# Attention output products of six units, each as three products of rounded operands

## The reference

```
xn  = layernorm(layernorm(x)) * g1 + b1
q   = xn @ Wq                          # 16 heads x 64
k,v = split(xn @ Wkv)                  # one head of 64 each
attn = softmax(q k^T / 8)              # per head, 512 x 512
out  = concat_heads(attn @ v)          # 512 x 1024
x = x + layernorm(out @ Wo) * g2 + b2  # Wo: 1024 x 128
x = x + moe(layernorm(x))              # top 2 of 8 experts, F = 512
```

## Time and profile before

| | us |
|---|---|
| median of 3 executions | 604.21 (603.86 to 606.01) |
| profiled execution | 605.66 |
| span of its trace | 603.7 |

### The profile page before, as it was taken

One profiled execution on the slowest core, in us unless ns is written; L12 is line 12 of the kernel. 1 busy time (PEld: TensorE's weight loads), 2 busy tenths in 40 slices (PEclk: granted clock), 3 DMA queues, 4 the chain that ended last, 5 costly groups with the idle time before them and its releaser, 6 DMA issues. The chain is left out here.

```text
span 603.7 us, 8807 instructions
## 1 busy us (share of the span) xinstructions
PE 571.4 (95%) x2543; PEld 326.3 (54%) x2543; DVE 399.3 (66%) x875; ACT 297.8 (49%) x559; POOL 393.8 (65%) x329
## 2 busy tenths in 40 slices
PE   8799999999999999998999999899998898899992
PEld 6464455444545554444545545444443577788882
DVE  4878656657756869774567777876485458444463
ACT  3235655545636564463556445355635564355541
POOL 6448776667758866798598568949745944345332
PEclk9889999999999999998999999999998999999997
DMA  5111012010201200062000000000004410231042
GB/s 167 71 72 71 2 71 75 0 73 1 75 1 72 74 2 1 7 233 81 1 3 2 1 1 25 16 2 3 11 0 119 119 31 23 58 91 47 19 141 89
DMA packets 27805, 29.46 MB, mean 49 GB/s; under 512 B 7763, under 2 KB 19285, under 8 KB 27760
## 3 DMA queue, kind: packets, MB, share of 16 engines
q1 hardware_dynamic: 25056, 24.27, 12.5%
q0 software_dynamic: 2272, 4.24, 2.1%
q10 hardware_dynamic: 432, 0.39, 0.2%
HBM read 13.50 MB, written 15.32 MB: 48 GB/s over the span
## 5 line engine op out<-in xcount | busy, mean ns | idle before, releaser
L1203 ACT ACTIVATE prob<-s_ps 128x512 f32<-128x512 f32 x256 | 150.8, 599 | 183.3 <-PE s_ps L1300 180.9
L1123 DVE TENSOR_REDUCE less_max<-max_ps 128x1 fp32r<-128x512 f32 x256 | 174.0, 689 | 81.0 <-PE max_ps L1278 78.6
L1049 POOL TENSOR_TENSOR fold<-prob 128x1024 f32<-128x1024 f32 x63 | 149.6, 2375 | 88.7 <-ACT prob L1203 88.0
L1314 PE MATMUL pv_ps<-prob,v 128*64 128x512 f32 x512 | 138.5, 621 | 0.0
L1298 PE MATMUL s_ps<-q_hl,khh 128*128 128x512 f32 x256 | 117.9, 460 | 0.7 <-ACT prob L1203 0.7
L1278 PE MATMUL max_ps<-khh,q_hl 128*128 128x512 f32 x256 | 103.0, 408 | 5.4 <-DVE less_max L1123 4.8
L1300 PE MATMUL s_ps<-q_hm,kly 65*128 65x512 f32 x256 | 101.9, 398 | 0.0
L1298 PEld LDWEIGHTS s_ps<-q_hl,khh 128*128 128x128 f32 x256 | 48.6, 190 | 85.8 <-ACT prob L1203 67.1
L1055 POOL TENSOR_TENSOR psums<-fold 128x512 f32<-128x512 f32 x63 | 80.8, 1282 | 4.9
L1278 PEld LDWEIGHTS max_ps<-khh,q_hl 128*128 128x128 f32 x256 | 49.1, 192 | 23.4 <-DVE less_max L1123 11.1
L1300 PEld LDWEIGHTS s_ps<-q_hm,kly 65*128 65x128 f32 x256 | 48.8, 191 | 9.2 <-issue 3.3
(11 more groups left out here) (252 smaller groups left out, 772.0 us busy)
## 6 DMA issues: line engine op xcount, KB each, us to landing
sorted_rows<-raw_w SPq DMA_DIRECT2D x36, 260.0 KB, 2.6
raw_w<-in_gate_upT SPq DMA_DIRECT2D x8, 512.0 KB, 8.5
wd<-in_downT SPq DMA_DIRECT2D x8, 256.0 KB, 4.1
raw_w<-parts SPq DMA_DIRECT2D x6, 256.0 KB, 3.4
psums<-sorted_rows SPq DMA_DIRECT2D x22, 65.0 KB, 1.9
...
```

The lines of the kernel that those rows point to most:

```text
L1049: nc.gpsimd.tensor_tensor(fold[:, :, :], prob[:, head % 4, 0:2, :], prob[:, head % 4, 2:4, :], ALU.add).then_inc(prob_folded, 1)
L1123: nc.vector.tensor_reduce(less_max[:, group % 2, col:col + 1], max_ps[:, k % 2, :], AX_X, ALU.max, negate=True).then_inc(max_done, 1)
L1203: nc.scalar.activation(prob[:, head % 4, jt, :], s_ps[:, k % 2, :], ACT.Exp, scale=SCALE).then_inc(exp_done, 1)
L1314: last = nc.tensor.matmul(pv_ps[DH * hd:DH * hd + DH, :], v[:, b % 2, jt, :], prob[:, head % 4, jt, :], start=(jt == 0), stop=(jt == JT - 1))
```

## The change

For units 0 to 5 (24 of the 32 pairs) the OUT product is taken as three products of rounded operands (float32r), as Q is. Wo is split once into a high and a low part (`woh`, `wol`) by GpSimd, one of 8 pieces after each of the heads 2 to 9. In NORM, VectorE multiplies twice, first into `hl[:, 0]` (rounded, the high part) and then into `ao` (float32). A new step LOW on GpSimd subtracts the first from the second into `hl[:, 1]`. `ao` is free again when LOW has read it, so VectorE's NORM of pair k now waits for LOW of pair k-2. `hl` has three slots. NORM moves to slots 14, 16, 19, 21; LOW stands at 18, 18, 22, 22; OUT at 21, 23, 25, 27. Unit 6's NORM and OUT move to the same slots and keep the one float32 product; the last unit is as before. The new tiles lie over the place of the last four experts' `gate_up` weights, so these four are loaded after unit 5's last OUT.

```
-NORM_AT = (14, 17, 19, 22)
-OUT_LAG = 5
+NORM_AT = (14, 16, 19, 21)
+LOW_AT = (18, 18, 22, 22)
+OUT_AT = (21, 23, 25, 27)
+HL_SLOTS = 3
+FIRST_WEIGHTS = 4
+SPLIT_UNITS = 6
...
                 if k >= 2:
-                    dve.wait_ge(out_mm, k - 1)
+                    if k - 2 < SPLIT_UNITS * UP:
+                        dve.wait_ge(al_ready, k - 1)
+                    else:
+                        dve.wait_ge(out_mm, k - 1)
+                if u < SPLIT_UNITS:
+                    if k >= HL_SLOTS:
+                        dve.wait_ge(out_mm, k - HL_SLOTS + 1)
+                    nc.vector.tensor_tensor(hl[:, 0, k % HL_SLOTS, :], sum_ps[:, :], raw[:, k % RAW_SLOTS, :],
+                                            ALU.mult).then_inc(ah_ready, 1)
                 nc.vector.tensor_tensor(ao[:, k % 2, :], sum_ps[:, :], raw[:, k % RAW_SLOTS, :],
                                         ALU.mult).then_inc(ao_ready, 1)
...
+                slot = k % HL_SLOTS
+                if u >= SPLIT_UNITS:
+                    pe.wait_ge(ao_ready, k + 1)
+                    nc.tensor.matmul(y_ps[:, :], wof[:, c, :], ao[:, k % 2, :], start=c == 0,
+                                     stop=c == PAIRS - 1).then_inc(out_mm, 1)
+                else:
+                    pe.wait_ge(wo_split, min(k, PAIRS - 1) + 1)
+                    pe.wait_ge(ah_ready, k + 1)
+                    nc.tensor.matmul(y_ps[:, :], woh[:, c, :], hl[:, 0, slot, :], start=c == 0, stop=False)
+                    nc.tensor.matmul(y_ps[:, :], wol[:, c, :], hl[:, 0, slot, :], start=False, stop=False)
+                    pe.wait_ge(al_ready, k + 1)
+                    nc.tensor.matmul(y_ps[:, :], woh[:, c, :], hl[:, 1, slot, :], start=False,
+                                     stop=c == PAIRS - 1).then_inc(out_mm, 1)
...
-                        for e in range(E):
+                        for e in range(FIRST_WEIGHTS):
                             load_gate_up(sp, e)
+                    if (kind, u, a) == ("OUT", SPLIT_UNITS - 1, UP - 1):
+                        sp.wait_ge(out_mm, SPLIT_UNITS * UP)
+                        for e in range(FIRST_WEIGHTS, E):
+                            load_gate_up(sp, e)
...
+                        if 2 <= head < 2 + PAIRS:
+                            if head == 2:
+                                pool.wait_ge(wo_in, 16)
+                            part = head - 2
+                            link_pool(pool, nc.gpsimd.tensor_scalar(woh[:, part, :], wof[:, part, :], 1.0, 1.0, ALU.mult,
+                                                                    ALU.mult))
+                            nc.gpsimd.tensor_tensor(wol[:, part, :], wof[:, part, :], woh[:, part, :].bitcast(F32),
+                                                    ALU.subtract).then_inc(wo_split, 1)
+                    if kind == "LOW":
+                        k = u * UP + a
+                        slot = k % HL_SLOTS
+                        if k >= HL_SLOTS:
+                            pool.wait_ge(out_mm, k - HL_SLOTS + 1)
+                        pool.wait_ge(ao_ready, k + 1)
+                        pool.wait_ge(ah_ready, k + 1)
+                        nc.gpsimd.tensor_tensor(hl[:, 1, slot, :], ao[:, k % 2, :], hl[:, 0, slot, :].bitcast(F32),
+                                                ALU.subtract).then_inc(al_ready, 1)
```

26 lines of the change are left out of this document (16 added, 10 removed).

## The result

The changed kernel takes 612.81 us (median of 6, 610.76 to 613.96) against 603.84 (median of 6, 602.38 to 606.01) for the kernel before on the same chip: ratio 1.0136, 95% interval 1.0117 to 1.0155, so slower. By the two profiled executions it is 612.48 against 605.66, by their spans 610.7 against 603.7. The forecast, 607.9, had the side and not the size, and the time lies above its range (up to 611.5).

The account below looks back on a forecast made before the run. TensorE was taken to bound the kernel, working 372.1 of 378.0 us. Terms -3.4 (20 OUTs), +0.8 (unit 2), +3.0 (unit 4) and +3.3 (unit 6) gave +3.7: 607.9 us against the median 604.21, 8-in-10 range 600.3 to 611.5.

Parts of the forecast that it names:

- TensorE's gain: Three rounded products take 0.70 us where the float32 product takes 0.87, so each of 24 OUTs gains 0.17, 4.1 in all.
- the new places change nothing in this: Moving the OUTs to new slots, all behind PV, leaves TensorE's gain of 0.17 us an OUT as it is.
- the term of -3.4: The gain of the 20 OUTs outside the two stopped stretches, 0.17 us each, 3.4 us saved.
- no cost where VectorE doesn't wait: VectorE's 24 added products of 0.69 us, 16.6 in all, are hidden by its idle time: 113 of 378 us.
- Unit 2: XL up to 0.9 us later delays LOW; VectorE done at 166.8, TensorE needs it at 166.1: +0.8 us, bounds 0 and 1.6.
- Unit 4: First LOW behind XL and SEND stops OUT 1 and NORM 4, half clock one stretch later: slot 24 at 284.6, +3.0 us.
- Unit 6: First LOW behind a late SEND stops OUT 1 and NORM 4, then LIST0 stops MAX 23: slot 24 at 393.3, +3.3 us.
- The third, 2.3 for LIST0: In unit 6 LIST0 meets GpSimd's fold, pushed later by LOW, and TensorE stands 2.3 us before MAX 23.
- I take 0: A fall of the clock in unit 6 would cost about 1.6 us, bounds 0 and 3.2; it was counted as 0.
- Unit 7: No cost was counted for the moved NORM and OUT of unit 6's pairs, which run here: 0 us.
- Rival C: Larger stops: clock fall in unit 6 (+1.6), VectorE's two-input steps held up more by GpSimd (+2): 611.5 us, chance 0.10.
- Rivals A and B: A: LOW comes in time in units 4 and 6, 600.1 us, chance 0.17. B: one stop is hidden, 604.3, chance 0.28.

Follow-up runs that it names:

- e9: The changed kernel without LOW (the third product reads the high part again) and with NORM and OUT at the old slots: ratio 0.9942 to the kernel before.
- e4: The changed kernel's new slots with one float32 product everywhere, no LOW, four ao buffers, split of Wo and late loads kept: ratio 1.0084 to the kernel before.
- e5: The changed kernel with NORM and OUT of unit 6's pairs, which run in unit 7, back at the old slots: ratio 1.0126 to the kernel before.
- e14: The changed kernel with LIST0 of unit 6 at slot 25 instead of 20 and LIST1 at 27: ratio 1.0138 to the kernel before.
- e1: The changed kernel with four ao buffers instead of two for the pairs of units 0 to 5: ratio 1.0144 to the kernel before.
- e3: The changed kernel with the third product rereading the high part and GpSimd doing an equal-sized subtraction for LOW that no computing engine awaits: ratio 1.0073.
- e11: The changed kernel with the first LOW ahead of the SEND of slot 17 in units 4 and 6: ratio 1.0114 to the kernel before.
- e16: The kernel before, unchanged, run and profiled once more: ratio 0.9986.

## Why the prediction was right and where it was wrong

- **TensorE's gain, 0.17 an OUT.** The price is right: -0.6 for the four OUTs of unit 2 in e9, 0.16 each. The Trainium skill (FP8 and Floating Point Precision, TensorE Precision Notes) has true FP32 as 4 passes; an estimate by that is 0.22 each and -0.9, and the measurement decides against it. Wrong was "the new places change nothing in this", and with it the term of -3.4 for the 20 OUTs outside the stops. Units 1, 3 and 5 of the changed kernel have -0.4, -0.2 and -0.2, not -0.7 each: 12 OUTs gave 0.8 us instead of 2.0. The places alone cost 0.1 to 0.3 in each of units 1, 2, 3 and 5 (e4). And "no cost where VectorE doesn't wait" isn't so: TensorE waits 0.34 and 0.42 for a maximum in units 3 and 5, which it doesn't with one product (before, e4) and does at the old places too (0.36 and 0.43, e9).
- **Unit 2.** The stop was forecast at +0.8 (its own times, 166.8 and 166.1, give 0.7) with the gain outside it, so +0.1 net; +0.8 came. The place was right (NORM 4 and what follows it); without LOW the unit has -0.3, so the stop cost 1.2 and the gain was half of the forecast's.
- **Unit 4, +3.0 with two OUTs' gain outside it, so +2.7 net.** Right, in place, mechanism and nearly in size: +3.0 came. Counted from slot 12, slot 22 came 3.7 later than before (forecast 3.4), slots 22 and 23 took 3.3 and 2.2 (3.3 and 2.3), and slot 24 came 3.3 later (3.0). The clock fell at 274.9, earlier than I let it: the half clock lasted twice as long as before, and about half of its first 3.4 us lay in the stops. At that clock TensorE came to OUT 1's third product later and stood 0.83 for LOW, where my times give 1.1, and the NORM behind it took 0.56 instead of 0.33.
- **Unit 6, +3.3, so +3.0 net.** Mechanism and both first stops right: 1.9 and 1.2 forecast, 1.71 and 1.08 measured. The third, 2.3 for LIST0, didn't come, and not because LIST0 was quicker: VectorE ended it 21.0 us after slot 12, where I had 21.2. TensorE ran at half clock from 387.6 on, 0.5 us behind the first stop, so it came to MAX 23 only at 22.2, after the maximum. "I take 0" for the clock was wrong: up to 3.4 us by the windows above. It took the place of the third stop, so in sum it cost little more than forecast: +3.7, nearly right in sum and half wrong in its parts.
- **Unit 7, nothing.** This step was wrong, +1.1. Unit 6's pairs keep the float32 product, which frees `ao` only when it ends, and OUT 1 now stands at slot 21 right ahead of NORM 4. So TensorE stands for 0.98 while VectorE makes `ao`. I had followed only the six units whose product changes; the seventh had its places changed too. e5 gives it back, and e4 has it without any LOW.
- **The sum.** Forecast +3.7; the seven units give +7.8. By unit the misses are: units 1, 3, 5 +1.3, unit 2 +0.7, unit 4 +0.3, unit 6 +0.7, unit 7 +1.1, together 4.1. So the steps that failed are, by size, the gain taken as unchanged at the new places (1.6, with its share of unit 2), the wait of unit 7 put at nothing (1.1), the clock put at 0 in unit 6 (that unit 0.7) and the size of unit 2's stop (0.4). The medians lie 9.0 apart, for the profiled execution of before was 1.8 over its median; its start (1.1 to 2.0 slower than in 11 of the 19 later profiles, and 0.3 to 0.5 slower than in three) is part of that.
- **Rival C** named the fall of the clock in unit 6 and VectorE's held steps. I gave it 0.10 and priced it at 3.6 over the forecast. The fall came; the held steps cost nothing in the changed kernel (e14), but did in e1, e3, e4 and e11. It named neither the places nor unit 7. How much was clock: over all runs of each kernel the mean granted clock is 0.9775 for the changed kernel (6 runs, mean span 610.9) and 0.9839 for the kernel before (12 runs of e16, mean span 603.5). Span times clock is 597.2 and 593.8. With the other sets of runs of the kernel before (five, 17 to 29 runs each) it is 594.4 to 595.3. So, as an estimate, 2 to 3.4 us are work and waits and 4 to 5.5 the clock; this is an upper bound for the clock, since half clock costs nothing where TensorE stands.
- **Rivals A and B** fail: GpSimd wasn't early, and neither stop was hidden.
- **A reading.** The waits that I called the only ones of note leave out one of 1.4 us for VectorE's `psums`. It lies behind the last score, is in both kernels, and changes nothing in the sum.

What stays open: the part behind the attention moves by up to 2.5 us between profiles, of one kernel too (1.5), with falls of the clock at 452 to 526 us in some of them; how much of the rest of e3's and e11's share there is theirs wasn't separated. Open too: what decides whether the clock falls after a stand, and why units 1, 3 and 5 keep less than 0.17 an OUT even in e9 beyond the waits named.
